# One turn of the attention in another order: the first maximum tile before the projection

## The reference

```python
y = jnp.einsum('bnd,hde->bhne', x, Wkqv) + bkqv[None, :, None, :]   # x is the layernorm of the input
k, q, v = y[..., :Dm], y[..., Dm:2 * Dm], y[..., 2 * Dm:]           # k, q: 128 wide; v: 8 wide
A = jnp.einsum('bhnd,bhmd->bhnm', q, k) / jnp.sqrt(jnp.float32(Dm))
A = jnp.where(mask[None, None], A, -jnp.inf)                        # causal
A = jax.nn.softmax(A, axis=-1)
sa = jnp.einsum('bhnm,bhmd->bnhd', A, v).reshape(Bm, Nm, Dm)
return sa @ Wp + bp
```

## Time and profile before

| | us |
|---|---|
| median of three runs | 948.55 |
| lowest and highest | 947.72, 948.93 |
| the profiled execution | 948.73 |
| its span, first to last instruction | 946.5 |
| PE busy | 854.0 (90%) |
| DVE busy | 613.4 (65%) |
| ACT busy | 526.0 (56%) |
| POOL busy | 321.1 (34%) |

### The profile page before, as it was taken

One profiled execution on the slowest core, in us unless ns is written; L12 is line 12 of the kernel. 1 busy time (PEld: TensorE's weight loads), 2 busy tenths in 40 slices (PEclk: granted clock), 3 DMA queues, 4 the chain that ended last, 5 costly groups with the idle time before them and its releaser, 6 DMA issues. The chain is left out here.

```text
span 946.5 us, 16760 instructions
## 1 busy us (share of the span) xinstructions
PE 854.0 (90%) x5342; PEld 562.8 (59%) x5342; DVE 613.4 (65%) x1838; ACT 526.0 (56%) x914; POOL 321.1 (34%) x452
## 2 busy tenths in 40 slices
PE   6466999999999999999999986659999999999996
PEld 6342555454545455454545445657888888888884
DVE  4976676666766676666766615857666666666665
ACT  3321666666666566666666562226565555555554
POOL 2130121211212121211212123406666666666664
PEclk9775999999999999999999999659999999999999
DMA  8000000000000000000000000005514434544503
GB/s 207 0 1 0 2 2 2 2 1 2 1 2 2 2 3 1 2 1 3 1 1 2 2 2 1 0 27 78 102 39 87 66 76 78 70 73 78 77 2 89
DMA packets 52672, 28.11 MB, mean 30 GB/s; under 512 B 4297, under 2 KB 52577, under 8 KB 52609
## 3 DMA queue, kind: packets, MB, share of 16 engines
q1 hardware_dynamic: 52608, 27.29, 15.7%
HBM read 24.93 MB, written 2.36 MB: 29 GB/s over the span
## 5 line engine op out<-in xcount | busy, mean ns | idle before, releaser
L598 ACT ACTIVATE p_sb<-bank,inv_scale 128x512 f32<-128x512 f32 (+1 forms) x384 | 222.1, 614 | 130.8 <-PE bank L538 127.7
L641 DVE CUSTOM_DVE_ANT_0 junk<-bank,causal 128x512 bf16<-128x512 f32 (+3 forms) x512 | 224.5, 484 | 71.9 <-PE bank L520 71.9
L493 POOL TENSOR_SCALAR_AFFINE_SELECT p_sb<-p_sb 128x384 f32<-128x384 f32 x128 | 66.6, 520 | 404.2 <-ACT p_sb L598 404.2
L1073 DVE TENSOR_TENSOR gu<-bank,sg 128x512 f32<-128x512 f32 x144 | 99.5, 691 | 100.3 <-ACT sg L1018 100.3
L537 PE MATMUL bank<-ql,ah 128*128 128x512 f16 (+3 forms) x512 | 153.4, 300 | 0.0
L538 PE MATMUL bank<-qh,al 128*128 128x512 f16 (+3 forms) x512 | 152.9, 300 | 0.0
L520 PE MATMUL bank<-ah,qh 128*128 128x512 f16 (+3 forms) x512 | 135.8, 310 | 15.6 <-DVE low L641 11.5
L617 DVE TENSOR_TENSOR ql<-bank,qh 128x512 f16<-128x512 f32 x128 | 88.5, 692 | 92.1 <-ACT qh L590 92.1
L536 PE MATMUL bank<-qh,ah 128*128 128x512 f16 (+3 forms) x512 | 147.1, 300 | 0.0
L944 POOL TENSOR_TENSOR gul<-gu,guh 128x512 fp32r<-128x512 f32 x72 | 98.6, 1370 | 139.0 <-DVE yw L1063 107.7
L1018 ACT ACTIVATE sg<-bank 128x512 f32<-128x512 f32 x144 | 86.3, 599 | 104.7 <-PE bank L986 104.1
(11 more groups left out here) (165 smaller groups left out, 1238.5 us busy)
## 6 DMA issues: line engine op xcount, KB each, us to landing
wbc<-w_dram SPq DMA_DIRECT2D x8, 2048.0 KB, 28.8
wst<-in_Wkqv SPq DMA_DIRECT2D x8, 264.0 KB, 5.0
x_sb<-in_x SPq DMA_DIRECT2D x8, 256.0 KB, 5.9
out<-x_sb SPq DMA_DIRECT2D x8, 256.0 KB, 2.4
wraw<-in_gate_w SPq DMA_DIRECT2D x8, 128.0 KB, 27.9
wraw<-in_up_w SPq DMA_DIRECT2D x8, 128.0 KB, 10.3
wraw<-in_down_w SPq DMA_DIRECT2D x8, 128.0 KB, 8.9
c_dram<-lowT SPq DMA_DIRECT2D x32, 4.0 KB, 1.3
```

The lines of the kernel that those rows point to most:

```text
L598: nc.scalar.activation(p_sb[v % P_RING][:, S_AT[k]:S_AT[k] + S_WIDTH[k]], m.psum[S_BANK[k]][:, 0:S_WIDTH[k]], ACT.Exp, scale=m.inv_scale[: ...
L641: last = nc.vector.tensor_tensor_reduce(out=junk[:, (3 * u + k) % 2, at:at + w], in0=m.psum[M_BANK[(3 * u + k) % 2]][:, at:at + w], in1=m. ...
L1073: nc.vector.tensor_tensor(gu[par][:, k, :], m.psum[UB[k]][:, :], sg[:, k, :], ALU.mult).then_inc(gu_ready, 1)
```

## The change

In a turn PE now makes maximum step 0 of unit t-1 before it projects unit t, and no longer between score 0 and score 1. On DVE the read of that step comes first in the turn, ahead of ql; the reads of steps 1 and 2 stay behind ql, lowT and o_sb. The body of the read has become a function, reduce_max. Instructions, waits and their values are the same.

```diff
@@ PE @@
                     nc.tensor.transpose(m.psum[T_BANK][:, 0:P], low[g % 2][:, :], m.ident[:, :]).then_inc(low_T, 1)
+                if 0 <= t - 1 < UNITS:
+                    score_for_max(t - 1, 0)
                 if t < UNITS:
                     project(t)
                 if (g := group_at(t, PV_AT)) is not None:
...
                 for k in range(3):
                     if 0 <= t - LAG < UNITS:
                         score(t - LAG, k)
-                    if 0 <= t - 1 < UNITS:
+                    if k >= 1 and 0 <= t - 1 < UNITS:
                         score_for_max(t - 1, k)
@@ DVE @@
+            def reduce_max(u, k):
+                g, r = divmod(u, GROUP)
+                if k == 0 and g < 2 and r == 0:
+                    dve.wait_ge(low_clear, 2)
+
+                if k == 0 and g >= 2 and r == 0:
+                    dve.wait_ge(low_T, g - 1)
+                dve.wait_ge(max_scored, 3 * u + k + 1)
+                for i, at in MAX_TILES[k]:
...
+                last.then_inc(max_ready, 1)
+
             for t in range(SLOTS):
+                if 0 <= t - 1 < UNITS:
+                    reduce_max(t - 1, 0)
                 if t < UNITS:
                     dve.wait_ge(qh_ready, t + 1)
...
-                u = t - 1
-                if 0 <= u < UNITS:
-                    g, r = divmod(u, GROUP)
...
-                    for k in range(3):
-                        dve.wait_ge(max_scored, 3 * u + k + 1)
...
-                        last.then_inc(max_ready, 1)
+                if 0 <= t - 1 < UNITS:
+                    reduce_max(t - 1, 1)
+                    reduce_max(t - 1, 2)
```

More of the change, by code:

```diff
@@ L610, in _ @@
             nc.vector.memset(m.psum[O_BANK][:, :], 0.0).then_inc(o_clear, 1)
+            def reduce_max(u, k):
[6 more added lines that the diff above has]
+                for i, at in MAX_TILES[k]:
+                    w = (i + 1) * P
+                    last = nc.vector.tensor_tensor_reduce(out=junk[:, (3 * u + k) % 2, at:at + w], in0=m.psum[M_BANK[(3 * u + k) % 2]][:, at:at + w], in1=m.causal[:, N - w:N], scale=-1.0 / (KAPPA * LIFT), scalar=-MASKED,
+                                                          op0=ALU.add, op1=ALU.min, accum_out=low[g % 2][:, r * TB + i:r * TB + i + 1])
+                last.then_inc(max_ready, 1)
             for t in range(SLOTS):
+                if 0 <= t - 1 < UNITS:
+                    reduce_max(t - 1, 0)
                 if t < UNITS:
```

## The result

The changed kernel takes 998.77 us (median of four runs, 995.61 to 999.95) against 948.65 for the kernel before: a ratio of 1.0525, with a 95% interval of 1.0499 to 1.055. It is slower by 50 us. The forecast was 991.0 in a range of 980 to 1002.

A forecast was written before the change was run, and what follows sets the result against it. The prediction took PE to bound the attention's body. New head waits less waits removed gave 38.1 + 2.2 + 0.6 - 0.8 + 2.4 = +42.5 us, so 991.0 us, range 980 to 1002.

The forecast's parts named there:

- Each head waits for the read of step 1: At a turn's first matmul, PE waits for DVE's read of the previous unit's second maximum tile, same bank: 0.60 us.
- The waits of 0.12 and 0.32: PE's old waits at the third maximum tile, in plain turns and those with lowT; claimed to go.
- the one for oT: PE's old wait of 0.48 us at the oT transposes, once per four turns; claimed to go.
- ql's lateness: On DVE, ql comes later by the first tile's 0.215 us; claimed that nobody wants it before score ten turns later.
- the 0.09 worked out: Margin in us by which DVE finishes lowT before the second maximum tile is readable, in turns with lowT.
- Turn 128 and the tail: Turn 128 has no project, so its head's 0.60 isn't paid: claimed -0.8 us.
- the head doesn't wait: Rival: the second tile's read is done before the next head; -18 us, about 930; chance 0.06.
- in some heads only: Rival: the new wait is paid in two of four heads, time about 956; chance 0.05.
- 0.06 after the release: Handover term of the head's wait: PE starts 0.06 us after DVE frees the bank.
- a slower handover: Upper bound for the head's wait: handover like ACT's 0.42 after PE instead of DVE's, giving 0.70 us.
- The first ten turns and turn 10: Turns 1 to 9, without scores, claimed +2.4 us; turn 10, the first with scores, +0.6.
- The clock's rival: Rival: standstills drop PE to its lower clock level; for half the time, about 1200 us; chance 0.03.

The follow-up runs named there:

- e4: Changed kernel with the contents of maximum steps 1 and 2 exchanged, so step 1 is the 256 column tile alone: 945.84 us, ratio 0.9963.
- e3: Changed kernel with PE's wait for qh of a turn moved ahead of score 2 of the turn before: 990.18 us, ratio 1.0431.
- e5: Changed kernel with maximum step 1 ahead of score 1 on PE instead of behind it, DVE's list untouched: 965.81 us, ratio 1.0187.
- e1: Kernel before with PE's half of the change only, step 0 ahead of project; DVE's list as before: 1033.28 us, one run.
- e7: Kernel before with maximum step 2 one turn later, behind project on PE, its read ahead of ql on DVE: 922.37 us, ratio 0.9726.
- e6: Changed kernel with the edits of e3 and e4 together: 937.23 us, ratio 0.9878.
- e8: The kernel of e7 with the transposes of oT moved behind score 0 on PE: 904.90 us, ratio 0.954.

## Why the prediction was right, and where it was off

**The mechanism** held at each step. Each head waits for the read of step 1 (e4 cuts the wait from 0.69 to 0.23 by that step's size alone). The waits of 0.12 and 0.32 are gone, and so is the one for oT. The third step doesn't wait. ql's lateness costs nothing, and lowT is covered, by the 0.09 worked out: its record starts at 434.87, and read 1 still starts 0.42 after its matmuls. Turn 128 and the tail came out within 0.3 us. The rival "the head doesn't wait" needed tile 1 read 0.6 us sooner, and nothing of that kind happened; "in some heads only" falls with 110 waits in 110 turns.

**The term that was mis-sized** is the release, "0.06 after the release", taken from the plain turn of the earlier trace rows. At a head it is 0.15, in 75 of 100 heads between 100 and 520 us and in the others within 0.01. That row belongs to a matmul with one wait, and the head's has two, the one for qh ahead; I said of the price that all its terms were "rows of exactly this tile and these engines", which wasn't so for this one. e3 measured the term: with the wait for qh moved away it is 0.07, and the kernel takes 990.2, against the 991.0 of the forecast. The forecast had "a slower handover" only as a bound of its range. Within a group, four times 0.09 less a PV and an OT turn shorter by 0.01 and 0.06 are the 0.28 by which it missed, 7.6 us over 28 groups. The same term made the wait at a head 0.69 instead of 0.60, near the upper end of the 0.50 to 0.70 that the range was made from.

**The first ten turns and turn 10** cost 5.1 instead of 3.0. The turns at the low clock are 4.05 as against 4.01, again the release. Most of the rest, 1.7, is in turns 1 and 2, priced "at full clock about +0.2 each": in the changed kernel they already take 4.03 and 4.05 us (60.29, 64.32 and 68.37 are their starts of project), where the kernel before took 2.96 and 3.02 for them at the higher clock. The row from 60 to 80 us shows it:

```profile
60.00:80.00 20.00, 12.33 (x35) 4.41 (x35) 11.88 (x45) 2.99 (x5) 7.16 (x1) 0.50 0.00 0
```

The mean granted clock there is 0.50; it was 0.67 before. The longer waits at the heads can't have caused this: the matmuls at 60.29 already have the records of the lower level (0.61 us), and the first such wait ends only at 63.94. Besides, e5, whose first ten turns are ordered as in the changed kernel, had 0.67. Why the clock fell earlier in this execution is open. Another 0.5 is in turn 10, which cost 1.1 and not 0.6: before, the clock rose 3.0 us after that turn's project began, here only after 3.9.

**The phase ahead of the attention** ended 1.65 us sooner, though nothing in it was changed. It ended at 59.71 in the kernel before, at 59.78 in e5 and 60.00 in e1, and at 58.06 to 58.72 in the changed kernel and the other five. The order in the attention doesn't sort these, so I don't count it as a gain of the change; it happened to bring the total nearer to the forecast.

**The clock's rival** didn't occur: 1.00 from 105 to 565 us, with PE standing still once a turn while two PSUM banks alternate. The rule cited for it, of the Trainium skill's "TensorE: Matmul & The Clock Gate", section "A second HAM failure mode: psum-queue depth-cycling", doesn't show here: with standstills of 0.69 us in turns of 3.50 the granted clock stayed at 1.00.

## What to carry to other kernels

Where steps alternate between two buffers, moving one of them earlier also moves it closer to the step before it in the ring: write down for each step how much of the engine's own work lies between it and the reader that frees its buffer, and compare that with the reader's time. A step that always waits may be better a turn late than half a turn early, if its reader has idle time there (e7). And take the price of a handover from an instruction with the same waits in the same order as the one in question; where a wait that is long met stands ahead of the one that holds, try it further up the list.

## What was not expected of the hardware

- A matmul with two waits, the first of them long met, starts 0.15 us after the other's release; with the first wait moved away it is 0.07 (e3), and in the kernel before it was 0.06 for a single wait. It was worth 0.30 us a group in e3 and 0.23 in e6. The transposes of oT, with three waits of which the first is the one that holds, start after 0.05. Why the wait ahead costs this is open: the records show the time only as "issue".
- The clock of the first ten turns went with the order. With turns of 3.6 to 4.7 us PE was granted 0.50 to 0.53 of its clock between 66 and 80 us (the kernel before, the changed one, e1, e3 to e6), with turns of 2.24 us and the same matmuls 1.00 (e7, e8). This isn't one lucky execution: the clock over the whole span was 0.959 to 0.965 in all eight runs of e7 and e8 and at most 0.950 in those of the kernel before. An order that only took a wait away came with the higher clock, and the ten turns took 11 us less where 6 were expected. The length of a single wait doesn't decide it: PE waited 1.17 us at a time in the kernel before and 1.55 in the changed one, but e6 was at 0.50 too, with three waits of 0.47 or less in a turn of 3.64. What does is open, since no run changes the waits alone.
